# Five banks for the first batch's scores, a split table preparation, separate load semaphores, and roundings of two batches on ScalarE

## The reference

```
# 1 attention: 16 heads of 16, plus 32 rotary features shared by all heads, causal
c_kv = x @ W_kv_down;  q = x @ W_q;  k = c_kv @ W_k_up;  v = c_kv @ W_v_up
scores = (q k^T + rot(x @ W_q_rope) rot(c_kv @ W_k_rope)^T) / sqrt(48), masked
y = softmax(scores) v @ W_o
# 2 ternary dense: weights rounded to {-1,0,1} times a row mean, plus a low-rank part
h = bitlinear(x, w_fc) + gate * (x @ v.T @ fast_b.T @ u.T)
y = bitlinear(relu(h)**2, w_proj)
# 3 memory mixer: 32 keys x 8 features, 8 angles each
z = x @ W_in;  k_val, s = causal conv of z;  phi = k_val * theta
p_w = exp(clip(scale*s) + log_tw)
den, re, im = cumsum(p_w), cumsum(p_w*cos(phi)), cumsum(p_w*sin(phi))
y = silu(combination of (re, im)/den with the queries) @ W_out
# 4 dense: relu(x @ W1 + b1) @ W2 + b2
```

## Time and profile before

| what | us |
| --- | --- |
| median of 3 runs | 1451.83 |
| lowest and highest run | 1449.29, 1453.98 |
| the profiled execution | 1458.32 |
| its span | 1456.5 |

### The profile page before, as it was taken

How to read it: one execution, slowest core, us unless ns; L and a number is a source line. 1 busy time by engine, 2 the same in 40 slices (tenths; PEclk the granted TensorE clock), 3 DMA queues, 4 the chain that set the end, 5 groups by cost and what they waited for, 6 DMA issues and landing times.

```text
span 1456.5 us, 22659 instructions
## 1 busy us (share of the span) xinstructions
PE 1239.4 (85%) x7820; PEld 778.7 (53%) x7820; DVE 1123.3 (77%) x2291; ACT 1031.5 (71%) x2069; POOL 334.0 (23%) x317
## 2 busy tenths in 40 slices
PE   4787988798889998999989997999899998974747
PEld 2465465455455665466646755556546665632424
DVE  3573439868879898889968996989888997979940
ACT  3565578658796979678886888598967888536522
POOL 2951401240014201241023201430133101410101
PEclk9797999799999998999999999999999999986959
DMA  7410423141315114151315221420414131021100
GB/s 234 102 23 1 103 43 101 48 115 47 87 44 131 37 29 126 43 124 23 101 33 140 49 83 51 107 60 23 133 37 110 29 104 42 31 79 60 37 0 15
DMA packets 72017, 101.48 MB, mean 70 GB/s; under 512 B 10640, under 2 KB 44064, under 8 KB 71904
## 3 DMA queue, kind: packets, MB, share of 16 engines
q1 hardware_dynamic: 71904, 100.03, 26.2%
HBM read 74.31 MB, written 25.69 MB: 69 GB/s over the span
## 4 chain that ended last, share of the span: by engine, by line
PE 58%; ACT 17%; DVE 15%; issue 7%; POOL 1%; DMA 1%; SPq 1%; POOLq 0%; DVEq 0%; ACTq 0%
PE ps L856 21%; PE ps L866 17%; PE ps L919 5%; DVE work L1465 5%; PE ps L937 4%; PE ps L1005 4%; PE ps L911 4%; DVE work L1388 4%; ACT work L1173 3%; ACT work L1166 3%; DVE work L1474 2%; ACT xnd L1109 1%; ACT work L1217 1%; ACT work L1221 1%; ACT work L1224 1%
## 5 line engine op out<-in xcount | busy, mean ns | idle before, releaser
L1465 DVE TENSOR_TENSOR_SCAN work<-work 128x512 f32<-128x512 f32 x256 | 313.0, 1256 | 32.2 <-ACT work L1221 28.6
L1166 ACT ACTIVATE work<-work 128x384 f32<-128x384 f32 (+3 forms) x512 | 264.8, 558 | 81.7 <-DVE work L1388 79.9
L1388 DVE CUSTOM_DVE_ANT_0 work<-ps,work 128x384 f32<-128x384 f32 (+3 forms) x512 | 228.2, 486 | 107.7 <-PE ps L911 102.7
L737 POOL TENSOR_TENSOR later_norms<-later_norms,singles 128x2 f32<-128x2 f32 x112 | 94.6, 845 | 717.6 <-ACT xnd L1109 465.1
L919 PE MATMUL ps<-ident,work 128*128 128x128 f32 x1280 | 202.1, 283 | 20.7 <-DVE work L1388 10.6
L919 PEld LDWEIGHTS ps<-ident,work 128*128 128x128 f32 x1280 | 150.6, 144 | 85.3 <-issue 36.0
L1173 ACT COPY work<-ps 128x512 f32<-128x512 f32 x300 | 170.3, 572 | 6.1 <-PE ps L919 5.9
L1474 DVE TENSOR_TENSOR work<-work 128x1024 f32<-128x1024 f32 x128 | 165.3, 1292 | 4.4
L911 PE MATMUL ps<-work 96*128 96x384 bf16 (+3 forms) x512 | 123.4, 308 | 22.3 <-ACT work L1173 14.6
L866 PE MATMUL ps<-wpr,hid 128*128 128x256 f32 x512 | 116.4, 387 | 5.2 <-POOL hid L757 5.2
L856 PE MATMUL ps<-led_xTd,wfc 128*128 128x512 f32 x256 | 120.1, 602 | 0.8 <-ACT led_xTd L1093 0.8
(11 more groups left out here) (173 smaller groups left out, 1955.7 us busy)
## 6 DMA issues: line engine op xcount, KB each, us to landing
work<-values SPq DMA_DIRECT2D x64, 256.0 KB, 3.2
work<-ratios SPq DMA_DIRECT2D x64, 256.0 KB, 4.4
scratch<-work SPq DMA_DIRECT2D x32, 384.0 KB, 4.4
work<-scratch SPq DMA_DIRECT2D x64, 192.0 KB, 3.9
work<-scratch SPq DMA_DIRECT2D x64, 128.0 KB, 4.2
x_in<-x SPq DMA_DIRECT2D x8, 512.0 KB, 6.7
work<-scratch SPq DMA_DIRECT2D x64, 64.0 KB, 4.3
values<-work SPq DMA_DIRECT2D x16, 256.0 KB, 3.2
```

The source lines that it names most:

```text
L737: g_.tensor_tensor(rstds[chain][:, tokens], spreads[chain][:, tokens], power[:, tokens], ALU.pow).then_inc(*rstd.one)
L1166: i = s_.activation(part_of, part_of, ACT.Exp, scale=-1.0, bias=nmax[:, row:row + 1])
L1388: i = v_.tensor_tensor_reduce(sc[:, n % 4, at:at + nk], out_of(b, name)[:, at:at + nk], base_of(qt), -SCORE_SCALE, BIG, ALU.add, ALU.min, ...
L1465: v_.tensor_tensor_scan(ring[:, at, m, :], pwr[:, slot, :], ring[:, at, m, :], 0.0, ALU.mult, ALU.add).then_inc(*scanned.one)
```

## The change

1. `plan_banks()` gives batch 0's `S`, `T` and `OT` five banks in rotation (0, 1, 2, 4, 5) instead of three.
2. `tables` is cut into five parts, each an item with a place of its own; `means` moves from the start of DVE's program to the end of preparation, and `out` of batch 0 waits for it there.
3. The loads have separate semaphores: `loaded_ident` for the identity, `loaded_wo` for `wo`, `loaded_first` for the others of the first loads. PE's first instruction waits only for the identity, its `ckv` of batch 0 for `loaded_first`; ACT waits for none of them. `smalls` is loaded after `wku`.
4. In batches 0 and 7 the eight `turn` items run on ACT (L1235 after the change: `Copy` with a scale, two of 128 x 512 for each turn) instead of DVE.
5. All word lists of `MERGE` are new.

```diff
-            "p": ... ["means"] + [("ternary", n) for n in range(4)] + [("prep", n) for n in range(16)] + ["tables"])}
+            "p": ... [("ternary", n) for n in range(4)] + [("prep", n) for n in range(16)] + [("tables", n) for n in range(5)] + ["means"])}
...
     "act":
-        "a5 p a2 p a2 p10 a34 p a5 p a4 p2 a5 p4 a49 d a d2 a6 d8 a3 d a4 d a4 d a6 d a3 d3 a5 d a7 d a5 d a6 "
+        "a7 p a2 p11 a51 p4 a6 p a3 p a6 p a14 p a17 d a d2 a6 d8 a3 d a4 d a4 d a6 d a3 d3 a8 d a4 d a5 d a6 "
...
+def turn_on_act(b):
+    return b in (0, B - 1)
...
-    last = {"a": 2, "d": 6}
+    last = {"a": 2, "d": 6, "first": 2}
...
+                if chain == "a" and b == 0 and item in ("S", "T", "OT"):
+                    last["first"] = (last["first"] + 1) % 5
+                    use(b, name, (0, 1, 2, 4, 5)[last["first"]])
+                    continue
...
             load_x(0)
-            first(ident[:], c_ident)
-            first(smalls[:], small)
+            sp.dma_start(ident[:], c_ident).then_inc(loaded_ident, 16)
...
             first(wku[:], w_k_up)
+            first(smalls[:], small)
...
-            first(wo[:], w_o.rearrange("(c p) n -> p c n", p=P))
+            sp.dma_start(wo[:], w_o.rearrange("(c p) n -> p c n", p=P)).then_inc(loaded_wo, 16)
...
-            pe.wait_ge(loaded_first, 16 * n_first[0])
+            pe.wait_ge(loaded_ident, 16)
...
                 if item == "ckv":
+                    if b == 0:
+                        pe.wait_ge(loaded_first, 16 * n_first[0])
...
                 if item == "out":
                     if b == 0:
-                        pe.wait_ge(prep_step, N_WO)
+                        pe.wait_ge(prep_step, N_PREP)
...
             act.wait_ge(values_blank, 2)
-            act.wait_ge(loaded_first, 16 * n_first[0])
...
+                if item == "turn" and turn_on_act(b):
...
+                    for m in range(MH):
+                        i = s_.activation(whole[:, COS_HALF[r], m, :], kvr[:, slot, :], ACT.Copy,
+                                          scale=turns[:, r, m:m + 1])
+                    i.then_inc(*rounded.one)
...
-                if item == "turn":
+                if item == "turn" and not turn_on_act(b):
...
-                if item == "tables":
+                if item == "tables" and n == 0:
                     prep(v_.tensor_scalar(wout[:], wout[:], 0.5, None, ALU.mult))
                     prep(v_.tensor_scalar(turns, turns, 1.0 / TWO_PI_EXACT, None, ALU.mult))
-
+                if item == "tables" and n == 1:
                     dve.wait_ge(prep_soft, 2)
...
                 if item == "means":
-                    dve.wait_ge(loaded_first, 16 * n_first[0])
+                    dve.wait_ge(loaded_wo, 16)
```

More of the change, by code:

```diff
@@ L153, in chains @@
             "m": sum((mixer_items(b) for b in range(B)), []),
-            "p": steps(0, ["means"] + [("ternary", n) for n in range(4)] + [("prep", n) for n in range(16)] + ["tables"])}
+            "p": steps(0, [("ternary", n) for n in range(4)] + [("prep", n) for n in range(16)] + [("tables", n) for n in range(5)] + ["means"])}
 PARTS = {
     "pe": "xT ckv q qr k kr v base S T PV OT attnT out fxT fc fproj zxT z total query gather oout gxT gc gproj prep",
-    "act": "ystats fstats fystats zstats oystats gstats gystats centre norm xT q k v S T PV attnT fnorm fxT fc znorm zxT z weights query fold cos sin silu gnorm gxT gc gsum ternary prep",
+    "act": "ystats fstats fystats zstats oystats gstats gystats centre norm xT q k v S T PV attnT fnorm fxT fc znorm zxT z weights query turn fold cos sin silu gnorm gxT gc gsum ternary prep",
     "dve": "stats ckv q qr k kr base S T OT sum fsum z weights ratio total rates turn frac scan mix gate silu "
@@ L1499, in _ @@
             count = [0]
+            e, ln, d, one = soft[:, 1, :], soft[:, 2, :], soft[:, 3, :], soft[:, 4, :]
             def prep(instruction):
@@ L1522, in prepare @@
                     k.then_inc(prep_drained[i], 1)
-                if item == "tables":
+                if item == "tables" and n == 0:
                     prep(v_.tensor_scalar(wout[:], wout[:], 0.5, None, ALU.mult))
                     prep(v_.tensor_scalar(turns, turns, 1.0 / TWO_PI_EXACT, None, ALU.mult))
+                if item == "tables" and n == 1:
                     dve.wait_ge(prep_soft, 2)
-                    e, ln, d, one = soft[:, 1, :], soft[:, 2, :], soft[:, 3, :], soft[:, 4, :]
                     prep(v_.tensor_scalar(d, e, 1.0, 1.0, ALU.add, ALU.subtract))
@@ L1531, in prepare @@
                     prep(v_.tensor_tensor(d, d, one, ALU.add))
+                if item == "tables" and n == 2:
                     prep(v_.reciprocal(d, d))
@@ L1534, in prepare @@
                     prep(v_.tensor_tensor(ln, ln, one, ALU.add))
+                if item == "tables" and n == 3:
                     prep(v_.tensor_tensor(ln, ln, e, ALU.mult))
```

16 lines of the change are left out of this document (13 added, 3 removed), and 85 rows, old and new, of the table MERGE.

## The result

| | median us | runs |
| --- | --- | --- |
| before (4 runs) | 1450.82 | 1449.29 to 1453.98 |
| after (4 runs) | 1415.69 | 1414.69 to 1416.25 |

The ratio is 0.9754, with a 95% interval from 0.9736 to 0.9773: 35 us or 2.5% shorter. The forecast was 14 us shorter (1438), in a range from 1427 to 1447. The direction was right, and the forecast gain was less than half of the measured one. Of all the runs in this document one execution of e5_turns took 1858 us, in a slow state with a mean granted clock of 0.64, and is left out.

What follows compares the result with a forecast made beforehand. The prediction took PE to bound the kernel most of the time, with stretches in which it waits. Its terms, -6.2 - 5 - 1 - 1.5 - 1.5 + 1.5 = -13.7, took 1451.8 to 1438 us, range 1427 to 1447.

Steps and rivals of the forecast that it cites:

- Start: Serial path to the first scores: earlier first loads and k pieces bring them at 45.1 instead of 51.3 us, -6.2.
- Attention of batch 0: Batch 0's attention: five banks shorten PE's waits and tables in parts free DVE, -5, from -1 to -9.
- Turns of batch 0: Mixer 0 beside attention 1: turns moved from DVE to ACT, -1 at the joint and -1.5 over the batch's rest.
- the +1: Turns of batch 0: the term would be +1 if ACT and not DVE set the pace.
- The middle: Repeating batches: new places of the mixer against attention, -0.3 per batch over five batches, -1.5, from -6 to +6.
- The last batches: Last two batches: gate 1 1.6 us earlier, batch 7's first scan later behind ACT's chain, +1.5, from -3 to +5.
- (b): Rival, whole kernel: everything pays, batch 0 -9, joint and batch 1 -5, middle -4, tail 0; -24, so 1428; chance 0.14.

Runs made afterwards that it cites:

- e5_turns: Changed kernel with the turns of batches 0 and 7 back on VectorE, each right before its fraction: 1421.72 us, ratio 0.9785.
- q3_wo: Changed kernel with ScalarE again waiting for the load of wo before its first instruction: 1420.89 us, ratio 0.978.
- q1_joint: Changed kernel with the second dense block's items at the joint of batches 2 to 6 back at their old places on TensorE and ScalarE: 1451.31 us, ratio 0.9985.
- h2_old_head: Kernel before up to the output of batch 0's attention, new lists from there on, turns on DVE: 1430.94 us, ratio 0.9849.

## Why the prediction was wrong

**Start: right for the first scores.** Forecast -6.2, first scores at 45.1; they came at 45.6 (-5.7). The k pieces were 1 us earlier than worked out, and PE's preparation, which the prediction did not look at, took that back. The wait for `wo` alone is worth 2.7 to 5.2 us, by the three ways of q3_wo. How much of the start arrives at the end is less sure: alone in the kernel before it brought 1.8 us, from 0 to 5.

**Attention of batch 0: too small by about half, for an incomplete reason.** Forecast -5, from -1 to -9. The two profiled executions differ by 11.0, the middles of the seven and five traces by about 10, and the shortest of each by 5.1. The reason named the banks, 7.7 us less a third. Removing them costs 9 to 11 and adding them alone brings about 2: the term was one of banks and of preparation's places together.

**Turns of batch 0: half of it.** Forecast -2.5, measured 4.5 to 6 for the turns of both batches, nearly all of it in batch 0's. The weighing of DVE's 136 against ACT's 116 busy us was right in sign. The rule that I cited from the Trainium skill (ScalarE: Activation LUTs, Rules for kernel authors), VectorE and not ScalarE for such arithmetic, is right here on the price: a pair took 1.33 us on ACT against 0.88 on DVE. Moving it still gained, so the +1 that stood beside that rule did not come.

**The middle: the step that failed.** "I price it at -0.3 per batch, five batches; bounds ... a tenth of the idle time each way." Measured: 4 us per period on average in the four like ones, where the prediction had named a period that differs by over 1.2 us as a sign of being wrong, and 21.0 (17 to 27 by the interval) for the new lists from batch 0's `out` on, tail included. The term was -1.5, from -6 to +6. The tenth came from no row. The rows to read were the waits that ended PE's idle time in a period, which the profile gives: in the four periods they name 7.7 us in front of `out`, 2.5 for the mixer's silu, 2.1 at the gather and 2.5 of issue. Of these 14.8 us, 12.2 are gone in the changed kernel, but they are picked with hindsight: the largest row, 11.5 in front of `PV`, hardly moved. The order of the changed kernel showed `gc` products moved in front of `out`, and the sums moved behind mixes. The forecast used three places of the order, two of them in the tail, where a few us were at stake, and none in the part that repeats seven times. "No work is removed" is true and has no weight: PE's busy time fell by 2.3 us in 632 and its idle time by 13.7.

**The last batches: right, as far as the traces tell.** Forecast +1.5, measured +2.3. Seven traces with the old tail's lists took 232.9 to 239.5 us there, those with the new ones 239.0 to 239.6, so a pair of single traces gives anything from -0.5 to +6.7. Gate 0 waited 14.99 us (forecast 13.5) and gate 1 to the first scan took 20.6 (forecast 20). No later scan waited for ACT, but two of DVE's fractions waited 3.6 us together for a turn on ACT:

```profile
1220.49 0.69 DVE L1502 TENSOR_TENSOR work<-ps,work 128x512 f32<-128x512 f32 x1 [14.99 <-PE ps L1017]
...
1284.39 2.34 DVE L1488 TENSOR_TENSOR_SCAN work<-work 128x512 f32<-128x512 f32 x2 [6.33 <-ACT work L1244]
```

POOL's squares beside an idle DVE took 1.0 us each, against 1.67 in the earlier trace rows:

```profile
1209.83 4.03 POOL L767 TENSOR_TENSOR hid<-hid 128x512 f32<-128x512 f32 x4
```

The Trainium skill (SBUF — State Buffer, "SBUF: two separate sides") says that the pair of ports which VectorE and GpSimd share is an exclusive lock, so that an operation of one can block one of the other. This pair of traces agrees: beside each other both took longer, POOL's square 1.67 instead of 1.01 us, DVE's turn 2.01 instead of 0.88.

**The rivals.** (b), everything pays, came nearest. Its 9 for attention of batch 0 was about right, but it too had only 4 us for the middle and ended at 1428. None had the middle as the main term.

What stays open: why the new middle is faster. Two kinds of placement are shown to matter in it, but how the gain divides among them and the many other items that moved is not known, and a wait that the new order covers was not isolated as its cause. The cuts could not tell it, since the cuts themselves cost time.

## What to carry to other kernels

When an order is rewritten throughout, begin with the part that repeats: list what ended the bound engine's idle time in one period, and look in the new order for what now stands in front of each of those waits. That sum, times the number of periods, is an estimate of the term's far end; here it would have been 14.8 us in four periods, or 26 in seven, where 17 to 27 were measured for the new order behind the head. A bound such as "a tenth of the idle time" is no reading. A placement is worth what its neighbours allow: moved alone in the old order, items of these kinds cost 9 to 28 us; put back alone in the new one, 22 to 25 and 34 to 37.

## What the runs showed of the hardware

PE's granted clock decides some microseconds in a way that no run here predicts. With the same 648 products, attention of batch 0 ran at a mean of 0.84 in one trace and of 0.93 in another, and the stage took 89.9 or 84.0 us. More idle time can come with a lower clock as well: q1_joint's matmuls of the middle took 17.3 us more at a mean clock of 0.95 instead of 0.97, beside as much again in idle time. A profiled stage should be compared with further traces of the same lists before a difference of 5 us is explained, and with several: the one trace h2_old_head would have halved the gain of batch 0's attention.
